# New preference tables for the order of one attention and feed-forward kernel

## The reference

```
x = x + causal_attention(layernorm(x))     # 16 heads of 16, biases, softmax(q k / 4) v, projection
x = x + ffn(layernorm(x))                  # hidden 768: silu(gate) * up, weights int32 / 127
x = x + sliding_attention(layernorm(x))    # window of 64 keys, 63 keys and values given ahead of token 0
x = x + ffn(layernorm(x))                  # the same weights
```

## Time and profile before

| | us |
|---|---|
| median of 3 runs | 1284.7 |
| lowest and highest | 1280.25, 1286.66 |
| profiled execution, first to last instruction | 1277.2 |
| PE busy | 1176.6 (92%) |
| DVE busy | 832.1 (65%) |
| ACT busy | 773.4 (61%) |
| POOL busy | 417.8 (33%) |

### The profile page before, as it was taken

How to read it: one execution, slowest core, us unless ns; L and a number is a source line. 1 busy time by engine, 2 the same in 40 slices (tenths; PEclk the granted TensorE clock), 3 DMA queues, 4 the chain that set the end, 5 groups by cost and what they waited for, 6 DMA issues and landing times.

```text
span 1277.2 us, 41722 instructions
## 1 busy us (share of the span) xinstructions
PE 1176.6 (92%) x17814; PEld 796.2 (62%) x17814; DVE 832.1 (65%) x1577; ACT 773.4 (61%) x1126; POOL 417.8 (33%) x406
## 2 busy tenths in 40 slices
PE   7999889998989999999998998999899999999988
PEld 5544378766854447876784444887677444587756
DVE  6898545555689945545759993555577998255553
ACT  5467945565646784567455677557654577755752
POOL 7522443213441323312343222431344213342142
PEclk9899989999999999999999999999999999999999
DMA  7431322544350041354343022144536204125431
GB/s 248 122 105 55 133 84 67 146 133 141 90 153 17 29 127 67 89 145 146 124 134 104 9 78 72 67 122 132 144 114 172 62 21 124 30 71 151 117 117 35
DMA packets 112282, 130.82 MB, mean 102 GB/s; under 512 B 32896, under 2 KB 92352, under 8 KB 111168
## 3 DMA queue, kind: packets, MB, share of 16 engines
q1 hardware_dynamic: 112096, 128.11, 33.8%
HBM read 46.21 MB, written 11.61 MB: 45 GB/s over the span
## 4 chain that ended last, share of the span: by engine, by line
PE 67%; ACT 10%; DVE 8%; SPq 4%; DMA 4%; issue 4%; POOL 3%; POOLq 0%; ACTq 0%; DVEq 0%
PE ring L1517 11%; PE ring L1483 8%; PE ring L1434 7%; ACT probs_causal L1244 5%; PE ring L1557 5%; PE ring L1558 5%; DVE peak L1044 5%; PE ring L1572 4%; PE ring L1577 4%; DMA on_lo<-onf 3%; SPq L1765 2%; PE ring L1487 2%; PE ring L1391 2%; PE ring L1392 2%; PE ring L1393 2%
## 5 line engine op out<-in xcount | busy, mean ns | idle before, releaser
L1044 DVE TENSOR_REDUCE peak<-ring 128x2 f32<-128x128 f32 (+3 forms) x448 | 384.6, 903 | 72.4 <-PE ring L1440 36.7
L1244 ACT ACTIVATE probs_causal<-ring 128x1024 f32<-128x1024 f32 (+1 forms) x320 | 286.8, 943 | 135.4 <-PE ring L1483 127.1
L1434 PE MATMUL ring<-k_st,q_st 96*32 96x512 bf16 (+15 forms) x3072 | 185.2, 320 | 21.2 <-DVE peak L1044 12.6
L1483 PE MATMUL ring<-q_st,k_st 98*32 98x512 bf16 (+3 forms) x3072 | 174.0, 328 | 16.6 <-ACT probs_causal L1244 11.6
L943 POOL TENSOR_TENSOR h_lo<-hid,h_hi 128x512 fp32r<-128x512 f32 x96 | 123.4, 1299 | 180.3 <-ACT h_hi L1297 180.2
L931 POOL TENSOR_SCALAR_AFFINE_SELECT probs_causal<-probs_causal 128x512 f32<-128x512 f32 x128 | 82.8, 650 | 304.1 <-ACT probs_causal L1244 303.8
L1517 PE MATMUL ring<-probs_causal,V 128*32 128x512 f32 (+3 forms) x1536 | 159.8, 492 | 5.0 <-POOL probs_causal L931 2.9
L1557 PE MATMUL ring<-xt_hi,w_gu_sb 128*128 128x512 f32 x384 | 153.2, 399 | 5.7 <-DVE xt_lo L975 5.2
L1558 PE MATMUL ring<-xt_lo,w_gu_sb 128*128 128x512 f32 x384 | 151.1, 394 | 0.0
L937 POOL TENSOR_TENSOR onf<-onf,o_hi 128x512 fp32r<-128x512 f32 x64 | 83.6, 1310 | 203.2 <-ACT o_hi L1264 202.9
L1434 PEld LDWEIGHTS ring<-k_st,q_st 96*32 96x32 bf16 x3072 | 72.4, 96 | 122.8 <-DVE peak L1044 47.3
(11 more groups left out here) (136 smaller groups left out, 2206.5 us busy)
## 6 DMA issues: line engine op xcount, KB each, us to landing
q_st<-q_part SPq DMA_DIRECT2D x192, 128.0 KB, 2.4
w_gu_sb<-img_gu SPq DMA_DIRECT2D x56, 384.0 KB, 4.3
k_st<-k_part SPq DMA_DIRECT2D x96, 144.0 KB, 2.5
k_st<-k_part SPq DMA_DIRECT2D x96, 128.0 KB, 2.4
w_qkv<-img_qkv SPq DMA_DIRECT2D x7, 1536.0 KB, 6.4
on_hi<-o_hi SPq DMA_DIRECT2D x64, 128.0 KB, 2.8
on_lo<-onf SPq DMA_DIRECT2D x64, 128.0 KB, 3.1
y<-X SPq DMA_DIRECT2D x8, 512.0 KB
```

Of the source, the lines that this page charges most:

```text
L1044: dve.tensor_reduce(dst, scores, AX.X, ALU.max).then_inc(a_max, 1)
L1244: act.activation(block[0:rows, n % slots, h:h + heads, 0:w], heads_of(flat_of(a, e), unit, w)[0:rows], ACT.Exp).then_inc(exp_done, 1)
L1434: pe.matmul(psum[32 * h:32 * h + 32, c:c + d], queries[0:SP_ROWS, head, block - HALF * hf:block - HALF * hf + 32], keys[0:SP_ROWS, head, W ...
L1483: last = pe.matmul(psum[32 * b:32 * b + 32, per * n:per * n + w], keys[:, head, first_key + 32 * b:first_key + 32 * b + 32], these, start= ...
```

## The change

The start of the diff, in its own form:

```diff
 LIKES = (
-    dict(turn=3.38, ahead0=0.38, ahead1=1.59, lead0=4.37, lead1=-1.34, late=1.22, Q=0.72, q=2.25, S=1.96, E=2.27,
-         P=0.7, A0=1.97, A1=1.07, N0=2.35, N1=2.18, T0=3.07, T1=2.87, B0=-0.71, B1=-0.53, V0=-0.77, V1=-0.68,
...
+    dict(turn=2.96, ahead0=0.36, ahead1=1.58, lead0=19.07, lead1=-14.17, late=1.14, Q=1.05, q=83.3, S=0.22,
+         E=0.79, P=-1.08, A0=3.45, A1=1.13, N0=2.1, N1=23.33, T0=2.3, T1=2.6, B0=-0.66, B1=-0.55, V0=-0.75,
...
```

More of the change, by code:

```diff
@@ L67 @@
-    dict(turn=3.43, ahead0=2.73, ahead1=-0.94, lead0=1.48, lead1=2.38, late=-0.66, Q=1.09, q=-1.01, S=-0.54,
-         E=1.16, P=2.43, A0=2.65, A1=-0.33, N0=1.15, N1=3.36, T0=-0.53, T1=-1.37, B0=0.9, B1=-0.14, V0=-2.22,
-         V1=-2.96, C0=0.41, C1=-0.19, R0=-1.1, R1=-3.36, M0=-1.88, M1=-5.93, H0=-2.56, H1=0.89, K0=-1.76,
-         K1=-4.75, O=-2.68, Y=-6.03, W=-4.34, Z=4.2, L=2.09, G=-5.33, I=-5.32, J=-1.54, D=-3.59, Ua=0, Uc=0, Ub=0,
-         Ud=0, Ue=0, Uf=0, Ug=0, F=-3.28, x=5.26, g=1.95, i=0.25, j=4.55, w=2.06, k=2.69, X=2.06),
@@ L77 @@
-    dict(turn=3.43, ahead0=2.73, ahead1=-0.94, lead0=1.48, lead1=2.38, late=-0.66, Q=1.09, q=-1.01, S=-0.54,
-         E=1.16, P=2.43, A0=2.65, A1=-0.33, N0=1.15, N1=3.36, T0=-0.53, T1=-1.37, B0=0.9, B1=-0.14, V0=-2.22,
-         V1=-2.96, C0=0.41, C1=-0.19, R0=-1.1, R1=-3.36, M0=-1.88, M1=-5.93, H0=-2.56, H1=0.89, K0=-1.76,
-         K1=-4.75, O=-2.68, Y=-6.03, W=-4.34, Z=4.2, L=2.09, G=-5.33, I=-5.32, J=-1.54, D=-3.59, Ua=0, Uc=0, Ub=0,
-         Ud=0, Ue=0, Uf=0, Ug=0, F=-3.28, x=5.26, g=1.95, i=0.25, j=4.55, w=2.06, k=2.69, X=2.06))
+    dict(turn=2.96, ahead0=0.36, ahead1=1.58, lead0=19.07, lead1=-14.17, late=1.14, Q=1.05, q=83.3, S=0.22,
+         E=0.79, P=-1.08, A0=3.45, A1=1.13, N0=2.1, N1=23.33, T0=2.3, T1=2.6, B0=-0.66, B1=-0.55, V0=-0.75,
+         V1=-0.7, C0=-0.8, C1=-0.68, R0=-1.34, R1=-0.07, M0=0.18, M1=-1.6, H0=-1.73, H1=-2.28, K0=16.42, K1=57.57,
+         O=-3.33, Y=-2.16, W=-0.09, Z=6.28, L=1.08, G=-2.31, I=73.51, J=-1.8, D=-4.93, Ua=29.89, Uc=17.5, Ub=33.9,
+         Ud=24.51, Ue=-24.85, Uf=-26.38, Ug=105.96, F=55.31, x=5.19, g=1.08, i=109.58, j=0.88, w=0.11, k=9.11,
+         X=-51.76),
@@ new lines @@
+    dict(turn=3.05, ahead0=42.53, ahead1=-0.28, lead0=-47.74, lead1=-47.22, late=1.02, Q=0.04, q=-3.01, S=-0.27,
+         E=13.88, P=0.08, A0=2.8, A1=1.4, N0=-0.04, N1=18.77, T0=-0.18, T1=-0.9, B0=1.21, B1=13.54, V0=-1.52,
+         V1=-0.34, C0=58.63, C1=48.36, R0=-1.3, R1=-1.75, M0=-1.63, M1=-1.98, H0=-2.13, H1=36.81, K0=100.78,
+         K1=-3.62, O=0.34, Y=-3.02, W=-2.81, Z=29.5, L=0.31, G=-0.9, I=-4.32, J=143.02, D=-2.06, Ua=-47.81,
+         Uc=21.1, Ub=-28.56, Ud=78.52, Ue=19.98, Uf=22.83, Ug=103.31, F=-3.68, x=33.65, g=0.07, i=4.21, j=0.05,
+         w=1.17, k=1.44, X=7.94),
@@ new lines @@
+    dict(turn=2.51, ahead0=1.53, ahead1=1.6, lead0=-40.6, lead1=-43.9, late=-1.52, Q=0.43, q=0.04, S=0.15, E=0.45,
+         P=1.1, A0=3.43, A1=1.15, N0=-0.45, N1=36.09, T0=2.01, T1=2.09, B0=-0.56, B1=-0.54, V0=-0.7, V1=-0.64,
+         C0=-0.88, C1=-0.61, R0=-1.31, R1=-1.07, M0=0.28, M1=127.61, H0=-1.26, H1=-1.85, K0=1.25, K1=24.3,
+         O=-2.39, Y=-1.15, W=77.9, Z=0.26, L=0.68, G=-3.6, I=94.94, J=-3.55, D=20.2, Ua=0.47, Uc=-0.56, Ub=-0.1,
+         Ud=-1.75, Ue=29.32, Uf=-0.5, Ug=114.21, F=9.41, x=74.28, g=-12.39, i=57.15, j=-36.12, w=35.78, k=72.35,
+         X=-84.5),
@@ new lines @@
+    dict(turn=3.5, ahead0=32.15, ahead1=-2.81, lead0=-34.45, lead1=2.58, late=-3.02, Q=2.33, q=-3.1, S=20.85,
+         E=20.33, P=1.95, A0=4.71, A1=-1.75, N0=0.46, N1=51, T0=-1.02, T1=-3.08, B0=-0.88, B1=2.93, V0=-4.05,
+         V1=-2.62, C0=34.45, C1=55.39, R0=-3.37, R1=-4.45, M0=-3.32, M1=-4.92, H0=-4.42, H1=93.76, K0=5.16,
+         K1=-6.62, O=-5.18, Y=-5.81, W=-4.91, Z=111.88, L=2.78, G=-4.24, I=-5.29, J=43.46, D=-4.81, Ua=-26.79,
+         Uc=-78.72, Ub=-71.83, Ud=9.6, Ue=19.44, Uf=4.5, Ug=108.86, F=-6.22, x=-64.72, g=2.47, i=66.86, j=3.25,
+         w=0.29, k=69.39, X=-106.51))
```

8 lines of the change are left out of this document (removed).

## The result

The changed kernel takes 1300.9 us (median), 1.0129 times the kernel before [1.0082, 1.0176]. It is slower by 1.3%, where 1266.5 us was forecast; the range ended at 1289. The square brackets hold the 95% interval of the ratio. A second measurement of the same kernel on another occasion gave 1300.87 us and 1.0117 [1.0080, 1.0155].

What follows compares the result with a forecast made beforehand. TensorE was taken as the bound, busy 1176.6 of 1277.2 us, with only idle and filler to win: 7.5 + 3 + 4.5 + 3 = 18 us off gives 1259.2, plus 7.5 is 1266.7, rounded to 1266.5 us; range 1246 to 1289.

Steps and rivals of the forecast that it cites:

- hardly move: Causal table: said of the entries ranking the bulk of the work; the large new numbers are on steps with little competition.
- The sliding tails, -2.5 us each: Tails of layers 1, 3, 5: waits for rank shorten and holes fill; 2.5 us off each, 7.5 in all.
- within 0.5 us of its statistics: Sign of being right: the layernorm's square root (std) on ScalarE starts within 0.5 us of its statistics.
- The last layer, -3: Layer 7: the same tail as sliding layers, now with its own table; bounds -1.2 to 10 us, 3 taken.
- The causal layers, -1.5 each: Layers 2, 4, 6: little slack on VectorE and TensorE; bounds -1.2 to 5 us, 1.5 taken each, 4.5 in all.
- The last "wrong" sign in the prediction: Sign of being wrong: the causal layers give more than the sliding ones.
- Layer 0, -3: Layer 0: core of the table stays, set-up steps get new ranks; bounds -3 to 8 us, 3 taken.
- its least likely case (0.04): Rival, TensorE's clock: shorter holes lose fillers, 14 more falls of 1.7 us cost 24 us, 1290 us; chance 0.04.
- a mean clock under 0.98: Sign that the rival of a falling TensorE clock holds: mean granted clock under 0.98.
- Table loads: ScalarE: a root between two exponentials costs two loads, 2.6 us of an engine busy for 61% of the span.
- SyncE's queue (rival 3): Rows of maxima stand behind early-planned packings in SyncE's queue; at 16 uncovered delays 1297 us; chance 0.08.

Runs made afterwards that it cites:

- experiment 7: experiment 3 with the root's table load behind the last h_hi split in every layer and no fillers ahead of L3 in sliding layers: 1289.9 us, 1.0036.
- experiment 9: Old opening table, new causal, sliding and final tables, with the edits of experiment 3, experiment 6 and experiment 7: 1272.38 us, 0.9902 of the kernel before.
- experiment 10: experiment 9 with the old sliding table for layers 1, 3 and 5: 1272.51 us, 0.9896 of the kernel before.
- experiment 1: The changed kernel with the old causal and opening tables, so only the sliding and final ones new: 1292.21 us, 1.0067 of the kernel before.
- experiment 11: The kernel before, all old tables, with the edits of experiment 7 alone: 1282.47 us, 0.9982.
- experiment 3: The changed kernel with last transposes L3 planned ahead of the last down product in causal and opening layers: 1292.34 us, 1.0065 of the kernel before.
- experiment 4: The changed kernel with nine filler matmuls ahead of the first gate product of layers 1, 3, 5 and 7: 1295.67 us, 1.0096 of the kernel before.
- The mixes: experiment 9 and experiment 10, old and new tables combined with repairs to the order: 1272.38 and 1272.51 us.
- experiment 2: The changed kernel with the old sliding and final tables, so only the causal and opening ones new: 1296.36 us, 1.0083 of the kernel before.
- experiment 12: The changed kernel measured again, unaltered: 1300.87 us, 1.0117 of the kernel before.
- experiment 6: experiment 3 with the second half's first layernorm root behind the last exponential in causal layers, not the opening one: 1289.68 us, 1.0027 of the kernel before.
- experiment 5: The kernel before with the second half's first layernorm root behind the last exponential in causal and opening layers: 1287.35 us, 1.0015.
- experiment 8: experiment 3 with eight fillers ahead of the matmuls that wait for the root, in causal and opening layers: 1291.04 us, 1.0053 of the kernel before.

## Why the prediction was wrong

**The step that failed** is the frame of the sum: each layer's term was bounded by the slack inside the layer, and a loss by one late VectorE step of 1.2 us (causal layers "-1.2 to 5", taken as 1.5 of gain; those 1.2 us are one of the two copies that the hole is made of). The wait of a layer's first gate product for the layer before was put at nothing, without a reason. What the runs showed in its place: that product waits 2.46 us for both copies of the last transposes, behind four layers, and from O1 to the next layer this costs 1.6 us in each causal layer and 2.2 in layer 0, 7.0 us in all. The second term at nothing is the clock, which takes 6.4 us. The gains of the sum did not come at all in the sliding and last layers, and in the causal ones were spent again.

The planner works out a layer by itself and takes the next one's start as given. Its own length of a layer (Plan.us, the number it computes when the kernel is built) shows the trap: it goes from 188.5 to 186.0 us in layer 0, from 187.0 to 184.8 in a causal layer, from 124.7 to 123.9 in a sliding one and from 145.9 to 144.5 in the last, 13 us less over the eight layers, where 16 more were measured. In the same plan xt_lo of the last transposes is done 0.3 us ahead of the causal layer's end with the old table and 2.15 us behind it with the new one. I had read that the lower-case g steps run inside the next layer and had not asked what their first instruction waits for. The ranks of L and W were in the diff (causal L 0.84 to 1.08, W -0.96 to -0.09), and I passed over them with "hardly move". By the planner alone (no run has it) W's rank is the one that counts of the two: the new causal table with the old W puts the transposes ahead of the last down product again, with the old L it does not, and the old table with both new values keeps its order, so the other entries have their part.

**The sliding tails, -2.5 us each**: the mechanism held up to O1 and the term was wrong. M is ahead of I (the two shuffles of layer 3 start at 619.12 and 620.51, the first product behind them at 621.90), and O1 comes 1.8 us sooner. The root did not come within 0.5 us of its statistics: they end at 611.41 and std starts at 612.83, again behind a load, a split and a copy. And what O1 gained was lost behind O1, 1.1 us by the table load that stands before the last splits (experiment 7 shows this by taking it away: O1 to W0 5.5 to 4.2) and 1.1 in W0 to next G. There the fillers stand in the changed kernel, and with them gone TensorE waits as long for VectorE, which has the fourth statistics ahead of xt_lo (experiment 7); that moving them alone gives the 1.1 back was not tried. Net of the table: 0 once the load is moved (experiments 9 and 10). As it is, the new sliding and final tables together cost 4.0 us of the rest (experiment 1).

**The last layer, -3**: to its last matmul 145.2 us before and 145.5 after, so 0 and not 3 (the 2.1 us between the rows by layer are in its stores' tail and its edge). With the load moved it is 142.8 to 144.4 with the new table and 143.7 with the old one (experiment 11), so the gain seen there goes with the load and not with its table, which was never measured alone.

**The causal layers, -1.5 each**: the forecast's sign was right for the middle. Start to O0 is 132.5 to 133.2 us in the six causal layers of experiments 3 and 4, against 135.3 to 136.0 before, a gain of 2 to 3 us; I had taken 1.5 for the whole layer. In the profile of the changed kernel only layer 4 shows it (132.9); layers 2 and 6 (135.3 and 136.1) have a fall of the clock in this stretch. The gain was spent on the seam (1.6), on the stretch behind O0 (1.2) and on the falls. The last "wrong" sign in the prediction, causal layers giving more than sliding ones, is what experiment 9 shows (2.0, 2.1 and 3.6 us, the last two against layers in which the clock fell once before, and none in the sliding layers together).

**Layer 0, -3**: it got 6 us longer: 2.2 by the seam, 1.8 between O0 and L2, and 3.5 before O0, less the 0.9 before O1. Part of the 1.8 is the fall at 149.47 us, which lasts twice as long as most. The cause of the 3.5 is open. It is in all kernels with the new opening table (139.0 to 140.8 against 135.5 to 137.5). The chain that ended last runs, from 51.2 to 63.4 us, through 17 stacking transfers (L1769) issued one behind the other at 0.5 to 1.3 us each on SyncE's queue, and in the kernel before through TensorE and VectorE. But this is not the 3.5: TensorE's busy time is 0.5 us less than before between 44 and 68 us, 1.1 less before that and 0.9 less from 68 to 136 (fillers included). No run tells it apart. The mixes avoid it with the old table.

**The clock.** The prediction had 14 more falls as its least likely case (0.04) and gave a mean clock under 0.98 as its sign; the mean clock is 0.981 in the profile, so the sign did not quite come, there are 7 more episodes, and the clock costs 6.4 us over the means and 11.9 in the profile. It was right in kind and half right in size, but it was set against "holes get fewer", and what I did not see is that a hole changes in kind when its filler goes. The sum is made on a profile that was itself a quick one: 7.5 us were added to its span, where a span is mostly some 1.8 us under its own execution's time (1300.57 and 1298.8 in the profile after). At the root hole (one place in each of layers 0, 2, 4 and 6) the clock fell in all 16 layers of the changed kernel and of experiments 2, 3 and 4, in 6 of 8 in experiments 7 and 12 and in layer 0 of experiment 6: 23 of 25. With the old order it fell in 7 of 12 (before, experiments 1 and 11) and in layer 0 of experiments 9 and 10: 9 of 14. It fell in none of 17 where the root is late or the hole filled (experiments 5, 6, 8, 9 and 10). The Trainium skill's page "TensorE: Matmul & The Clock Gate" (section "HAM oscillation — how this bites in real kernels") has falls come from gaps in which PE waits for transfers. The earlier trace rows have such a one, but at the two holes of this document PE waits 2.2 and 2.5 us for ScalarE and VectorE, and the clock falls all the same. Nor is one long gap needed: at 678.57 us before, and at 384.99 and 1006.22 after, it fell where no idle time of TensorE in the 6 us ahead is over 1.0 us (in the rows of 2 us from 676, 382 and 1004 us it was busy for 1.02, 1.23 and 1.17 us). Those falls belong to no hole that the tables made.

**Table loads.** The prediction named the mechanism (a root between exponentials, two loads, 2.6 us of ScalarE) and put it at nothing, because ScalarE is busy for 61% of the span. In its own stretch ScalarE is busy for 21.1 of 24 us. That is the share that counts, and the loads hold up TensorE there: by 0.7 us a causal layer in the new order, and the fall of the clock behind the hole costs as much again or more (25.1 to 25.9 and 26.6). In the old order they held up nothing (experiment 5), so putting them at nothing was right for the kernel before and wrong for the one after. The number of loads (48 at this line before and after) was no sign of it; their place was. Each took 1.28 us, and the next instruction started 1.29 us behind its start. The Trainium skill's page "ScalarE: Activation LUTs" (section "What ACT_TABLE_LOAD costs") gives about 2.66 us with the drain. The measurement decides: a switch to a root and back is 3.0 us here, with the root in it.

**SyncE's queue (rival 3)** did not decide: TensorE's waits for q_st<-peak_b come to 5.9 us in sum after and 5.2 before.

## What to carry to other kernels

When a planner orders one stage at a time, read the first instruction of the next stage on the bound engine and ask what it waits for: an order that ends its own stage sooner can leave exactly that for last. A planner's own number (here 13 us less) is no evidence for what it leaves out. Price a step against the share of its engine in its own stretch, not over the span, and count what the planner does not know (here the table loads and the clock) at every place where a rank puts it. Judge tables of preferences one by one: of these four the causal one was a gain once its two defects were mended, the sliding one nothing, the opening one a loss by its layer's length (199.2 to 200.6 us unaltered, 190.5 to 195.1 with the old table), and the final one was never measured alone.

## What the runs showed of the hardware

- A hole of 2.2 us (3.2 in layer 0) on TensorE between busy stretches was followed by a fall to 1.2 GHz in 23 of 25 layers; a hole of 1.8 to 2.0 us at the same step, with fillers before it, in 9 of 14; the same stretch with eight fillers in the hole, in none of 4. A hole of 2.46 us at the seam was followed by one in 7 of 12, and with nine fillers in it in none of 4.
- Falls also came where TensorE had no idle time over 1.0 us in the 6 us ahead (678.57 us before, 384.99 and 1006.22 after).
- Most episodes cost 1.7 us (from windows of 0.67 and 0.50), whatever the hole; some twice that. What is lost varies from run to run and makes up much of the spread: from 5.1 to 20.6 us over the 25 executions of the kernel before beside experiments 1 to 4, where the rest varies from 1264.2 to 1271.2.
- Fillers kept the clock and cost nothing at their place: L3 to the next G is 3.5 us with and without nine of them, O0 to L2 25.1 us with eight of them and in layers without where the clock stayed up. Still the mean span gained less than the clock gave: in experiment 8 2.1 us for 7.0.
- A table load took 1.28 us on ScalarE, and two of them with the root between took 3.0. What that costs depends on what waits there: 0.7 us a layer in the new order, nothing in the old.
